# Attention stage of a two-layer graph network: one-hot products ahead of the sums on TensorE, weighing ahead of the logits on VectorE, the transposed one-hot made by ScalarE

## The chip, the cores and the metric

The kernel runs on one core of a Trainium2 chip. The metric is the device time of one execution, in microseconds (us); three executions of the kernel before lie between 6692.63 and 6696.04 us. The engines are TensorE (PE, with its weight loads as PEld), VectorE (DVE), ScalarE (ACT), GpSimd (POOL) and SyncE (SP), which only starts transfers. Each engine runs its own instructions strictly in the order in which they are written; they meet at semaphores alone.

## The reference, cut to what matters

Two graph layers run over 6250 nodes and 106250 edges that are sorted by their destination node. The change lies in the relational attention of the first layer:

```python
def rel_gat(W, a_s, a_d, b, mask):              # once for each of 4 edge types
    x = (node_inp @ W).reshape(N, H, D)         # H = 8 heads, D = 16
    es, ed = einsum(x, a_s), einsum(x, a_d)
    logit = leaky_relu(es[src] + ed[dst], 0.2)
    p = exp(logit - mx[dst]) * mask[:, None]    # mx: maximum over a node's edges
    den = segment_sum(p, dst)
    out = segment_sum(p / den[dst] * x[src], dst)
```

The kernel sums `p` and `p * x[src]` for each destination together and divides later.

## The kernel before

The program is a row of phases with a barrier behind each: `lists` (the schedule), `node_inputs`, `relation_maxima`, `node_maxima`, `relation_attention`, `node_update`, `edge_inputs`, `edge_messages`, `outputs`. The change is in `relation_attention` (L804 to L952), and there are two small moves in `lists` and `edge_inputs`.

`relation_attention` handles 1028 steps in 257 groups of four (`U` = 4). A step is one block of 128 edges against one window of 32 destination nodes; with 4 edge types a window has 128 keys (type and node), and an edge belongs to one key. `T.key` holds each edge's key. For a group j the engines do this:

- SP, `load` (L831): brings `keyrow` (the keys of the group's 512 edges, the same row in all 128 partitions) and four blocks of `xe` (source features and source logits).
- DVE, `spread` (L861): `keyT` = (`keyrow` equals the partition's number + 1), the transposed one-hot, 128 keys by 512 edges.
- PE, `expand` (L933): four products `keyT` by the window's row of `K.edm` (called `l_outside` in the trace, whose memory it reuses) into `dst_ps`: each edge gets its destination's logit and maximum. A product in float32 is two weight loads and two matmul passes in the trace, so a group has 8 of each.
- DVE, `select` (L867), in three steps: `logit` (L871), `leaky` (L874), `arg` (L879), reading `xe` and `dst_ps`.
- ACT, `exponentials` (L916): `p` = exp(`arg`) (L920). ACT also copies the group's keys (`keep`, L925), from which POOL makes the other one-hot, `keyhot` (L851).
- DVE, `weigh` (L881): `px` = `p` times `xe`.
- PE, `sums` (L943): four products `keyhot` by `px` into `sum_ps`.
- DVE, `add` (L890), once for each step: adds `sum_ps` to the window's row of `acc`.

Every engine's code is a loop over turns t. `pipeline(engine, groups, ring, [(skew, stage), ...])` makes a turn of the stages in the order of the list, each for group t minus its skew. So the order inside a turn is written by hand. Before, PE's turn is sums(t-3), expand(t-1). DVE's turn is written out in `tick` (L897): add(t-4, step 0), logit(t-2), add(t-4, 1), leaky(t-2), add(t-4, 2), arg(t-2), weigh(t-3), add(t-4, 3), spread(t-1). ACT's turn is keep(t), exponentials(t-2). Buffers between stages have four slots (`RG` = 4), the PSUM tiles `dst_ps` and `sum_ps` two.

Of the kernel before, what the change touches and what calls it, by code (L numbers as in the profile page):

```python
# [286 lines left out]
def lists(nc, K, T):  # L287

    with Phase(nc, "list") as ph:
# [54 lines left out]
        def _(sp):  # L344
# [18 lines left out]
            sp.wait_ge(s_st, 160)  # L363
            sp.wait_ge(s_made, KEY)
            sp.dma_start(T.key.rearrange("(p k) e -> p k e", k=KKC), key[:, :, :]).then_inc(s_st, 16)
            sp.wait_ge(s_st, 176)
# [437 lines left out]
def relation_attention(nc, K, T, acc):  # L804

    with Phase(nc, "att") as ph:
# [4 lines left out]
        keyrow = ph.sb("keyrow", [P, RG, U * P])  # L811
# [7 lines left out]
        px = ph.sb("px", [P, RG, U, XR])  # L819
# [3 lines left out]
        s_kr = [ph.sem(f"kr{b}") for b in range(RG)]  # L823
        s_key, s_kh, s_kT, s_dst, s_sc, s_arg, s_p, s_px, s_sum, s_acc = (
            ph.sem(n) for n in ("key", "kh", "kT", "dst", "sc", "arg", "p", "px", "sum", "acc"))
# [3 lines left out]
        @block.sync  # L829
        def _(sp):  # L830
            def load(j, b):  # L831
                e = registers(nc, sp, mybir.EngineType.SP, K.reg_ke, j * U, U, BLOCKS * P)
                if past(j, RG):
                    sp.wait_ge(s_kT, j - RG + 1)
                    sp.wait_ge(s_px, j - RG + 1)
                    settle(sp, K)
                sp.dma_start(keyrow[:, b, :], key[ds(j, 1), :].to_broadcast([P, U * P])).then_inc(s_kr[b], 16)
                for u in range(U):
                    sp.dma_start(xe[:, b, u, :], T.xe[ds(e[u], P), :]).then_inc(s_xe[b], 16)

            pipeline(sp, GROUPS, RG, [(0, load)])
# [15 lines left out]
        def _(dve):  # L857
# [23 lines left out]
            def weigh(j, b):  # L881
                dve.wait_ge(s_p, j + 1)
                if past(j, RG):
                    dve.wait_ge(s_sum, (j - RG + 1) * U)
                dve.scalar_tensor_tensor(px[:, b, :, :].rearrange("p u (h s) -> p (u h) s", h=H),
# [11 lines left out]
            def tick(t, h, has):  # L897
# [17 lines left out]
        def _(act):  # L915
# [11 lines left out]
            pipeline(act, GROUPS, RG, [(0, keep), (2, exponentials)])  # L927

        @block.tensor
        def _(pe):  # L930
# [303 lines left out]
def edge_inputs(nc, K, T, h1T):  # L1234

    with Phase(nc, "edgein") as ph:
# [10 lines left out]
        s_w, s_x, s_sd, s_norm, s_h, s_hT, s_hTs, s_ab, s_abs = (  # L1247
            ph.sem(n) for n in ("w", "x", "sd", "norm", "h", "hT", "hTs", "ab", "abs"))
# [473 lines left out]
def build(nc, T):  # L1722
# [4 lines left out]
    with Phase(nc, "k") as ph:  # L1727
# [6 lines left out]
        K.reg_w, K.reg_e = ph.sb("reg_w", [1, P * KC], I32), ph.sb("reg_e", [1, P * KC], I32)  # L1734
# [76 lines left out]
```

## Time and profile before

| what | value |
|---|---|
| median of 3 executions | 6694.62 us |
| the profiled execution's own time | 6689.12 us |
| its span, first to last instruction | 6686.9 us |
| attention loop, 1518.3 to 3013.8 us | 1495.5 us, 22% of the span |
| mean turn of the attention loop, 245 turns from 1560 to 2980 us | 1420 / 245 = 5.80 us |
| TensorE's granted clock in that loop | 0.50 of full speed |
| busy share there: PE, DVE, POOL, ACT | 64%, 45%, 40%, 7% |

All else in this document is taken from the profiled execution, which lies 5.5 us below the median of the timed ones; its own time is 2.2 us over its span. In the rows, a number in brackets at a row's end is the time for which the engine had been idle before it, with the instruction that released it. A wait for several semaphores is put down to whichever came last by the profile, so the name after `<-` can be a neighbour of the true one. Where two rows of one engine overlap, the second was issued before the first had drained.

### The profile page before, as it was taken

Reading aid. Unit: us, or ns where it says so; the run is one execution under the profiler, and the core shown is the slowest. Engines: PE = TensorE matmul, PEld = TensorE weight load, DVE = VectorE, ACT = ScalarE, POOL = GpSimd, SP = SyncE. Lnnn points to the kernel's source line nnn. Section 1 sums busy time; section 2 is a strip of 40 time slices with the busy share of each in tenths; the row PEclk is TensorE's granted clock in tenths of the full one; section 3 lists DMA queues with packets and bytes.
Section 4 is the critical chain, followed back from the end, with each engine's and each line's share of the span. In section 5 each row is a group of like instructions: output and inputs, shape, how many; then the busy total and the mean of one; then the engine's idle time right before and its main releaser. Section 6 shows DMA issues by size and latency. Waiting matters only on the chain. (4 is left out here: it accounts for less than half of the span.)

```text
span 6686.9 us, 101415 instructions
## 1 busy us (share of the span) xinstructions
PE 3841.0 (57%) x17939; PEld 2899.4 (43%) x17940; DVE 3444.8 (52%) x10929; ACT 898.4 (13%) x2786; POOL 4148.2 (62%) x3995
## 2 busy tenths in 40 slices
PE   0332222215666666662467777777677777777766
PEld 0221111115666666661434444444444444444446
DVE  4632222214444444448955665656566566556654
ACT  0210000000000000003331111111111111111111
POOL 3067777764444443434228888888888888888870
PEclk9855555555555555555688888888888888888888
DMA  1355555533333333332268788787778877787874
GB/s 49 117 137 145 142 145 145 145 83 97 95 96 96 97 97 96 95 89 101 50 181 169 165 170 169 165 170 167 168 165 169 170 167 169 169 167 166 171 151 127
DMA packets 917009, 908.21 MB, mean 136 GB/s; under 512 B 231003, under 2 KB 735099, under 8 KB 916759
## 3 DMA queue, kind: packets, MB, share of 16 engines
q0 software_dynamic: 238848, 434.00, 32.4%
q1 hardware_dynamic: 678119, 473.77, 26.3%
q14 instruction: 30, 0.25, 0.0%
q8 instruction: 12, 0.20, 0.0%
HBM read 656.68 MB, written 250.64 MB: 136 GB/s over the span
## 5 line engine op out<-in xcount | busy, mean ns | idle before, releaser
L1409 POOL DMA_INDIRECT sums<-msg_bsum,msg_sidx x928 | 1558.8, 1680 | 308.0 <-issue 268.9
L1551 PEld LDWEIGHTS msg_fwd_ps<-msg_onehot,msg_hid 128*128 128x128 f32 x3712 | 639.8, 224 | 1422.1 <-issue 1313.4
L1418 POOL DMA_INDIRECT msg_ga<-ab,msg_idx x928 | 951.4, 1025 | 390.7 <-issue 240.8
L851 POOL TENSOR_SCALAR att_keyhot<-k_ramp,att_keys 128x128 f32<-128x128 f32 x1028 | 602.3, 604 | 895.9 <-PE att_sum_ps L949 873.4
L1564 PE MATMUL msg_pre_ps<-msg_rw,msg_lt 128*128 128x512 f32 x1856 | 1110.2, 684 | 37.1 <-DVE msg_xs L1488 28.1
L1551 PE MATMUL msg_fwd_ps<-msg_onehot,msg_hid 128*128 128x64 f32 x3712 | 621.6, 298 | 819.0 <-DVE l_fwd L1470 814.3
L686 POOL DMA_INDIRECT max_xe<-rows,max_idx x832 | 800.1, 962 | 422.8 <-issue 253.3
L949 PE MATMUL att_sum_ps<-att_px,att_keyhot 128*128 128x136 f32 x2056 | 559.1, 454 | 537.4 <-DVE l_acc L895 521.5
L949 PEld LDWEIGHTS att_sum_ps<-att_px,att_keyhot 128*128 128x128 f32 x2056 | 478.3, 331 | 563.7 <-DVE l_acc L895 546.8
L1553 PE MATMUL msg_bwd_ps<-msg_hid,msg_same 128*128 128x256 f32 x1856 | 708.9, 469 | 0.0
L1522 ACT ACTIVATE msg_bsum<-msg_bwd_ps 128x256 f32<-128x256 f32 x928 | 356.2, 384 | 2564.5 <-PE msg_bwd_ps L1553 2550.1
L1495 DVE SCALAR_TENSOR_TENSOR msg_hid<-msg_xs 128x512 f32<-128x512 f32 x928 | 639.2, 689 | 0.1
L939 PEld LDWEIGHTS att_dst_ps<-l_outside,att_keyT 128*128 128x128 f32 x2056 | 473.8, 334 | 94.3 <-issue 94.3
L939 PE MATMUL att_dst_ps<-l_outside,att_keyT 128*128 x2056 | 444.4, 357 | 94.0 <-DVE att_keyT L865 94.0
L742 PE MATMUL max_mT_ps<-k_ident,max_m 128*32 128x128 f32 x832 | 194.0, 413 | 492.3 <-DVE max_m L699 492.3
L1487 DVE TENSOR_TENSOR msg_xs<-msg_pre_ps,msg_ga 128x256 f32<-128x256 f32 x928 | 390.6, 421 | 165.8 <-PE msg_pre_ps L1564 93.1
L895 DVE TENSOR_TENSOR l_acc<-l_acc,att_sum_ps 128x136 f32 x1028 | 303.1, 295 | 294.9 <-PE att_sum_ps L949 272.3
L1463 DVE TENSOR_SCALAR msg_sidx<-msg_rowf,k_trash 128x4 int32<-128x4 f32 x232 | 57.6, 248 | 760.5 <-DMA sums<-msg_bsum,msg_sidx 758.2
L1564 PEld LDWEIGHTS msg_pre_ps<-msg_rw,msg_lt 128*128 128x128 f32 x1856 | 388.1, 222 | 116.5 <-DVE msg_xs L1488 49.8
L1470 DVE TENSOR_TENSOR l_fwd<-l_fwd,msg_fwd_ps 128x128 f32 x928 | 261.5, 282 | 241.5 <-issue 224.9
L1488 DVE TENSOR_TENSOR msg_xs<-msg_pre_ps,msg_ga 128x256 f32<-128x256 f32 x928 | 385.2, 415 | 0.0
L712 DVE TENSOR_TENSOR_SCAN max_run<-max_begin,max_run,max_mT_ps 32x1024 f32<-32x1024 f32 x103 | 240.4, 2334 | 224.2 <-PE max_mT_ps L742 224.2
(260 smaller groups left out, 4807.6 us busy)
## 6 DMA issues: line engine op xcount, KB each, us to landing
msg_rw<-ab SPq DMA_DIRECT2D x928, 128.0 KB
att_xe<-xe SPq DMA_DIRECT2D x1028, 72.0 KB, 2.5
att_keyrow<-key SPq DMA_DIRECT2D x257, 256.0 KB, 3.5
xe<-max_xe SPq DMA_DIRECT2D x104, 576.0 KB, 3.5
msg_lt<-in_efT SPq DMA_DIRECT2D x928, 32.0 KB
msg_ga<-ab,msg_idx POOLq DMA_INDIRECT x928
sums<-msg_bsum,msg_sidx POOLq DMA_INDIRECT x928
rows<-node_rows SPq DMA_DIRECT2D x50, 288.0 KB, 2.4
```

The lines of the kernel that those rows point to most:

```text
L686: pool.indirect_dma_start(xe[:, b, u, :], None, T.rows, bass.IndirectOffsetOnAxis(ap=idx[:, b, u:u + 1], axis=0)).then_inc(s_xe[b], 16)
L851: pool.tensor_scalar(keyhot[:, b, u, :], K.ramp[:, 1:P + 1], keys[:, b, u:u + 1], None, ALU.is_equal).then_inc(s_kh, 1)
L939: last = pe.matmul(dst_ps[b % 2][:, u, :], keyT[:, b, u * P:(u + 1) * P], K.edm[:, ds(w[u], 1), :].rearrange("k a c -> k (a c)"), start=Tr ...
L949: pe.matmul(sum_ps[b % 2][u // 2][:, u % 2, :], keyhot[:, b, u, :], px[:, b, u, :], start=True, stop=True).then_inc(s_sum, 1)
L1409: pool.indirect_dma_start(T.sums[u % 2], bass.IndirectOffsetOnAxis(ap=sidx[:, b, u:u + 1], axis=0), bsum[:, b, u, :], None, compute_op=ALU ...
L1418: pool.indirect_dma_start(ga[:, b, u, :], None, T.ab, bass.IndirectOffsetOnAxis(ap=idx[:, b, u:u + 1], axis=0)).then_inc(s_ga[b], 16)
L1487: dve.tensor_tensor(xs[:, u % 2, 0:HID], pre_ps[u % 2][:, 0:HID], ga[:, b, u, HID:2 * HID], ALU.add)
L1488: dve.tensor_tensor(xs[:, u % 2, HID:2 * HID], pre_ps[u % 2][:, HID:2 * HID], ga[:, b, u, 0:HID], ALU.add).then_inc(s_x, 1)
L1495: dve.scalar_tensor_tensor(hid[:, b % 2, u, :], xs[:, u % 2, :], SLOPE1, xs[:, u % 2, :], ALU.mult, ALU.max).then_inc(s_hid, 1)
L1551: pe.matmul(fwd_ps[u % 2][:, q * WIN:(q + 1) * WIN], hid[:, b % 2, u, HID + q * P:HID + (q + 1) * P], onehot[:, b, u, :], start=True, stop ...
L1553: pe.matmul(bwd_ps[u % 2][:, :], same[:, b % 2, u, :], hid[:, b % 2, u, 0:HID], start=True, stop=True).then_inc(s_edge, 1)
L1564: pe.matmul(pre_ps[u % 2][:, :], lt[:, b, u, :], rw[:, b % 2, u, :], start=True, stop=True).then_inc(s_pre, 1)
```

## The change

1. PE's turn becomes expand(t-1), sums(t-3).
2. DVE's turn becomes add(t-4, 0), weigh(t-3), add(t-4, 1), logit(t-2), add(t-4, 2), leaky(t-2), add(t-4, 3), arg(t-2). `spread` is no longer on DVE.
3. ACT makes `keyT` in two passes: `away` = |part1 - keyrow|, then `keyT` = relu(1 - away), with the two biases read from a column of SBUF. The second waits for the first. ACT also issues the transfer of `keyrow`, which SP issued before. ACT's turn is load(t), keep(t), exponentials(t-2), spread(t-1).
4. `keyrow` and `px` have two slots in place of four, and `away` has one.
5. The tables `K.reg_w` and `K.reg_e` are loaded in `edge_inputs`, where they are next needed, and no longer in `lists`.

```diff
@@ lists, SP
-            sp.dma_start(K.reg_w[:, :], T.sched_w.rearrange("(a s) -> a s", a=1)).then_inc(s_st, 16)
-            sp.dma_start(K.reg_e[:, :], T.sched_e.rearrange("(a s) -> a s", a=1)).then_inc(s_st, 16)
@@ relation_attention, tiles
-        keyrow = ph.sb("keyrow", [P, RG, U * P])
+        keyrow = ph.sb("keyrow", [P, 2, U * P])
+        away = ph.sb("away", [P, U * P])
-        px = ph.sb("px", [P, RG, U, XR])
+        px = ph.sb("px", [P, 2, U, XR])
@@ SP, load
-                    sp.wait_ge(s_kT, j - RG + 1)
                     sp.wait_ge(s_px, j - RG + 1)
                     settle(sp, K)
-                sp.dma_start(keyrow[:, b, :], key[ds(j, 1), :].to_broadcast([P, U * P])).then_inc(s_kr[b], 16)
@@ DVE
-            def spread(j, b):
-                dve.wait_ge(s_kr[b], filled(j, b, RG, 16))
-                if past(j, RG):
-                    dve.wait_ge(s_dst, j - RG + 1)
-                dve.tensor_scalar(keyT[:, b, :], keyrow[:, b, :], K.part1[:, 0:1], None, ALU.is_equal).then_inc(s_kT, 1)
@@ DVE, weigh
-                if past(j, RG):
-                    dve.wait_ge(s_sum, (j - RG + 1) * U)
+                if past(j, 2):
+                    dve.wait_ge(s_sum, (j - 1) * U)
@@ DVE, tick
                 for u in range(U):
                     if has(4):
                         add(t - 4, slot(4), u, w[u])
-                    if has(2) and u < 3:
-                        select(t - 2, slot(2), u)
-                    if has(3) and u == 2:
+                    if has(3) and u == 0:
                         weigh(t - 3, slot(3))
-                if has(1):
-                    spread(t - 1, slot(1))
+                    if has(2) and u > 0:
+                        select(t - 2, slot(2), u - 1)
@@ ACT
-            pipeline(act, GROUPS, RG, [(0, keep), (2, exponentials)])
+            def load(j, b):
+                if past(j, 2):
+                    act.wait_ge(s_away, j - 1)
+                    settle(act, K)
+                act.dma_start(keyrow[:, b % 2, :], key[ds(j, 1), :].to_broadcast([P, U * P])).then_inc(s_kr[b % 2], 16)
+
+            def spread(j, b):
+                act.wait_ge(s_kr[b % 2], filled(j, b, 2, 16) if isinstance(j, int) else (j - b % 2) * 8 + 16)
+                if past(j, 1):
+                    act.wait_ge(s_kT, j)
+                act.activation(away[:, :], keyrow[:, b % 2, :], ACT.Abs, bias=K.part1[:, 0:1], scale=-1.0).then_inc(s_away, 1)
+                if past(j, RG):
+                    act.wait_ge(s_dst, j - RG + 1)
+                act.wait_ge(s_away, j + 1)
+                act.activation(keyT[:, b, :], away[:, :], ACT.Relu, bias=K.ones[:, 0:1], scale=-1.0).then_inc(s_kT, 1)
+
+            pipeline(act, GROUPS, RG, [(0, load), (0, keep), (2, exponentials), (1, spread)])
@@ PE
-            pipeline(pe, GROUPS, RG, [(3, sums), (1, expand)])
+            pipeline(pe, GROUPS, RG, [(1, expand), (3, sums)])
@@ edge_inputs, SP
+            sp.dma_start(K.reg_w[:, :], T.sched_w.rearrange("(a s) -> a s", a=1)).then_inc(s_reg, 16)
+            sp.dma_start(K.reg_e[:, :], T.sched_e.rearrange("(a s) -> a s", a=1)).then_inc(s_reg, 16)
```

How the built programs stand. ACT, one turn inside the attention loop, before: the copy of the keys, then the exponentials (L920) behind their wait for `att_arg`.

```order
L924 ISA
L925 ISA [waits att_kh]
L925 ACTIVATE att_keys<-l_key 128x4
L919 REGISTER_ALU [waits att_arg]
L920 ACTIVATE att_p<-att_arg 128x32 [waits att_px]
```

The same turn of ACT in the changed kernel:

```order
L920 ISA [waits att_away]
L920 DMA att_keyrow<-key 128x512
L913 REGISTER_ALU
L914 ISA [waits att_kh]
L914 ACTIVATE att_keys<-l_key 128x4
L909 ACTIVATE att_p<-att_arg 128x32 [waits att_px,att_arg]
L923 ISA
L926 ACTIVATE att_away<-att_keyrow,k_part 128x512 [waits att_kT,att_kr0]
L930 ACTIVATE att_keyT<-att_away,k_ones 128x512 [waits att_away,att_dst]
```

The two passes that make `keyT` stand behind the exponentials of the turn, and so behind their wait for `att_arg`.

PE, inside the loop, before: the wait for `att_px`, the four sums (L949), then the wait for `att_kT` and the first of four expansions (L939).

```order
L948 ISA [waits att_px,att_kh]
L949 MATMUL att_sum_ps<-att_px,att_keyhot 128x136 [waits att_acc] x2
L948 REGISTER_ALU
L949 MATMUL att_sum_ps<-att_px,att_keyhot 128x136 [waits att_acc] x2
L935 REGISTER_ALU
L939 ISA [waits att_arg,att_kT]
L939 MATMUL att_dst_ps<-l_outside,att_keyT 128x16
```

PE in the changed kernel, from the last expansion of a turn to the wait that opens the next turn:

```order
L944 ISA
L944 MATMUL att_dst_ps<-l_outside,att_keyT 128x16
L949 REGISTER_ALU
L953 ISA [waits att_px,att_kh]
L954 MATMUL att_sum_ps<-att_px,att_keyhot 128x136 [waits att_acc] x2
L953 REGISTER_ALU
L954 MATMUL att_sum_ps<-att_px,att_keyhot 128x136 [waits att_acc] x2
L940 REGISTER_ALU
L944 ISA [waits att_arg,att_kT]
```

The sums now stand behind the expansions of the same turn, and the wait for `att_kT` stands ahead of both.

DVE, one turn ahead of the loop, before:

```order
L895 TENSOR_TENSOR l_acc<-l_acc,att_sum_ps 128x136
L871 TENSOR_TENSOR att_logit<-att_xe,att_dst_ps 128x32 [waits att_xe1,att_dst]
L895 ISA [waits att_acc,att_sum]
L895 TENSOR_TENSOR l_acc<-l_acc,att_sum_ps 128x136
L874 SCALAR_TENSOR_TENSOR att_leaky<-att_logit 128x32 [waits att_sc]
L895 ISA [waits att_acc,att_sum]
L895 TENSOR_TENSOR l_acc<-l_acc,att_sum_ps 128x136
L879 TENSOR_TENSOR att_arg<-att_leaky,att_dst_ps 128x32 [waits att_p,att_sc]
L885 SCALAR_TENSOR_TENSOR att_px<-att_p,att_xe 128x544 [waits att_sum,att_p]
L895 ISA [waits att_acc,att_sum]
L895 TENSOR_TENSOR l_acc<-l_acc,att_sum_ps 128x136
L865 TENSOR_SCALAR att_keyT<-att_keyrow,k_part 128x512 [waits att_dst,att_kr2]
```

The same turn of DVE in the changed kernel:

```order
L886 ISA [waits att_acc,att_sum]
L886 TENSOR_TENSOR l_acc<-l_acc,att_sum_ps 128x136
L876 SCALAR_TENSOR_TENSOR att_px<-att_p,att_xe 128x544 [waits att_sum,att_p]
L886 ISA [waits att_acc,att_sum]
L886 TENSOR_TENSOR l_acc<-l_acc,att_sum_ps 128x136
L862 TENSOR_TENSOR att_logit<-att_xe,att_dst_ps 128x32 [waits att_xe1,att_dst]
L886 ISA [waits att_acc,att_sum]
L886 TENSOR_TENSOR l_acc<-l_acc,att_sum_ps 128x136
L865 SCALAR_TENSOR_TENSOR att_leaky<-att_logit 128x32 [waits att_sc]
L886 ISA [waits att_acc,att_sum]
L886 TENSOR_TENSOR l_acc<-l_acc,att_sum_ps 128x136
L870 TENSOR_TENSOR att_arg<-att_leaky,att_dst_ps 128x32 [waits att_p,att_sc]
```

`arg` is now DVE's last instruction of the turn, behind all four adds and the weighing.

## Rows read from the trace of the kernel before

**Rows 1.** Busy time in the stretch: length, PE, PEld, DVE, ACT, POOL, clock, DMA, GB/s.

```profile
1560.00:2980.00 1420.00, 904.89 (x3918) 879.87 (x3918) 632.71 (x2204) 95.53 (x490) 574.14 (x980) 0.50 0.36 96
```

**Rows 2.** Who waited for whom, 1560 to 2980 us: total us, times, longest.

```profile
ACT att_p L920 <- DVE att_arg L879: 1313.1, 245, 5.4
POOL att_keyhot L851 <- PE att_sum_ps L949: 846.9, 245, 3.6
PE att_sum_ps L949 <- DVE l_acc L895: 515.1, 245, 2.2
DVE att_logit L871 <- PE att_dst_ps L939: 507.2, 245, 2.1
```

**Rows 3.** One turn in order of time: start, length, engine, line, [idle before].

```profile
2207.40 0.48 DVE L865 TENSOR_SCALAR att_keyT<-att_keyrow,k_part 128x512 f32<-128x512 f32 x1
...
2207.52 1.86 PEld L949 LDWEIGHTS att_sum_ps<-att_px,att_keyhot 128*128 128x128 f32 x8 [2.29 <-DVE l_acc L895]
...
2208.94 0.30 DVE L895 TENSOR_TENSOR l_acc<-l_acc,att_sum_ps 128x136 f32 x1 [1.06 <-PE att_sum_ps L949]
2209.27 1.84 PEld L939 LDWEIGHTS att_dst_ps<-l_outside,att_keyT 128*128 128x128 f32 x8
...
2211.26 0.19 DVE L871 TENSOR_TENSOR att_logit<-att_xe,att_dst_ps 128x32 f32<-128x32 f32 x1 [2.02 <-PE att_dst_ps L939]
2211.47 0.29 DVE L895 TENSOR_TENSOR l_acc<-l_acc,att_sum_ps 128x136 f32 x1
2211.68 0.21 DVE L874 SCALAR_TENSOR_TENSOR att_leaky<-att_logit 128x32 f32<-128x32 f32 x1
...
2212.29 0.72 DVE L885 SCALAR_TENSOR_TENSOR att_px<-att_p,att_xe 128x544 f32<-128x544 f32 x1
2212.49 0.23 ACT L920 ACTIVATE att_p<-att_arg 128x32 f32<-128x32 f32 x1 [5.36 <-DVE att_arg L879]
2212.68 0.21 ACT L925 ACTIVATE att_keys<-l_key 128x4 f32 x1
2212.93 0.29 DVE L895 TENSOR_TENSOR l_acc<-l_acc,att_sum_ps 128x136 f32 x1
...
2213.22 0.33 SPq L837 DMA_DIRECT2D att_keyrow<-key  x1
2213.25 1.86 PEld L949 LDWEIGHTS att_sum_ps<-att_px,att_keyhot 128*128 128x128 f32 x8 [2.14 <-DVE l_acc L895]
```

**Rows 4.** ACT by group: shape, count, busy us, mean ns, idle before.

```profile
L1012 ACT ACTIVATE l_acc<-upd_tmp 128x512 f32 x44 | 27.7, 630 | 55.5 <-POOL upd_tmp L1003 55.5
L1308 ACT ACTIVATE edgein_h<-edgein_x,edgein_nmr,edgein_rstd 128x128 f32 x46 | 22.3, 484 | 0.0
L593 ACT ACTIVATE node_h<-node_x,node_rstd 128x128 f32 x46 | 18.0, 392 | 0.0
```

**Rows 5.** Timeline of the stage's start: keyT ahead of expansions, and logit ahead of leaky.

```profile
1522.35 0.88 DVE L865 TENSOR_SCALAR att_keyT<-att_keyrow,k_part 128x512 f32<-128x512 f32 x1 [4.46 <-DMA att_keyrow<-key]
...
1523.37 1.78 PEld L939 LDWEIGHTS att_dst_ps<-l_outside,att_keyT 128*128 128x128 f32 x8 [92.87 <-issue]
...
1528.49 0.19 DVE L871 TENSOR_TENSOR att_logit<-att_xe,att_dst_ps 128x32 f32<-128x32 f32 x1 [2.06 <-PE att_dst_ps L939]
1528.71 0.19 DVE L874 SCALAR_TENSOR_TENSOR att_leaky<-att_logit 128x32 f32<-128x32 f32 x1
```

**Rows 6.** Timeline of ACT in a later phase: an exponential and the instruction behind it.

```profile
3131.18 0.24 ACT L1203 ACTIVATE mix_ex<-mix_al 128x40 f32<-128x40 f32 x1 [2.36 <-DVE mix_al L1123]
3131.32 0.58 ACT L1187 ACTIVATE mix_gT<-mix_gT_ps 128x512 f32<-128x512 f32 x1
```

**Rows 7.** Timeline of the stage's end: an add that waits for the add before it.

```profile
3009.56 0.30 DVE L895 TENSOR_TENSOR l_acc<-l_acc,att_sum_ps 128x136 f32 x1 [0.21 <-DVE l_acc L895]
```

**Rows 8.** Timeline of the start of `edge_inputs`: ACT's first tile and its wait.

```profile
3352.94 0.88 ACT L1308 ACTIVATE edgein_h<-edgein_x,edgein_nmr,edgein_rstd 128x128 f32<-128x128 f32 x2 [12.92 <-DMA edgein_x<-x]
```

**Rows 9.** The page, transfers: tiles, queue, count, KB each, median us from issue to landing.

```profile
att_keyrow<-key SPq DMA_DIRECT2D x257, 256.0 KB, 3.5
```

More of the change, by code:

```diff
@@ L358, in _ @@
             settle(sp, K)
-            sp.dma_start(K.reg_w[:, :], T.sched_w.rearrange("(a s) -> a s", a=1)).then_inc(s_st, 16)
-            sp.dma_start(K.reg_e[:, :], T.sched_e.rearrange("(a s) -> a s", a=1)).then_inc(s_st, 16)
             sp.dma_start(K.reg_kw[:, :], T.ksched_w.rearrange("(a s) -> a s", a=1)).then_inc(s_st, 16)
             sp.dma_start(K.reg_ke[:, :], T.ksched_e.rearrange("(a s) -> a s", a=1)).then_inc(s_st, 16)
-            sp.wait_ge(s_st, 160)
+            sp.wait_ge(s_st, 128)
             sp.wait_ge(s_made, KEY)
             sp.dma_start(T.key.rearrange("(p k) e -> p k e", k=KKC), key[:, :, :]).then_inc(s_st, 16)
-            sp.wait_ge(s_st, 176)
+            sp.wait_ge(s_st, 144)
         @block.gpsimd
@@ L822, in relation_attention @@
         s_xe = [ph.sem(f"xe{b}") for b in range(RG)]
-        s_kr = [ph.sem(f"kr{b}") for b in range(RG)]
-        s_key, s_kh, s_kT, s_dst, s_sc, s_arg, s_p, s_px, s_sum, s_acc = (
-            ph.sem(n) for n in ("key", "kh", "kT", "dst", "sc", "arg", "p", "px", "sum", "acc"))
+        s_kr = [ph.sem(f"kr{b}") for b in range(2)]
+        s_key, s_kh, s_away, s_kT, s_dst, s_sc, s_arg, s_p, s_px, s_sum, s_acc = (
+            ph.sem(n) for n in ("key", "kh", "away", "kT", "dst", "sc", "arg", "p", "px", "sum", "acc"))
         block = ph.block()
@@ L882, in weigh @@
                 dve.wait_ge(s_p, j + 1)
-                if past(j, RG):
-                    dve.wait_ge(s_sum, (j - RG + 1) * U)
-                dve.scalar_tensor_tensor(px[:, b, :, :].rearrange("p u (h s) -> p (u h) s", h=H),
+                if past(j, 2):
+                    dve.wait_ge(s_sum, (j - 1) * U)
+                dve.scalar_tensor_tensor(px[:, b % 2, :, :].rearrange("p u (h s) -> p (u h) s", h=H),
                                          p[:, b, :, :].rearrange("p u h -> p (u h)").unsqueeze(2).to_broadcast([P, U * H, HW]),
@@ L948, in sums @@
                         pe.wait_ge(s_acc, (j - 2) * U + u // 2 * 2 + 2)
-                    pe.matmul(sum_ps[b % 2][u // 2][:, u % 2, :], keyhot[:, b, u, :], px[:, b, u, :],
+                    pe.matmul(sum_ps[b % 2][u // 2][:, u % 2, :], keyhot[:, b, u, :], px[:, b % 2, u, :],
                               start=True, stop=True).then_inc(s_sum, 1)
-            pipeline(pe, GROUPS, RG, [(3, sums), (1, expand)])
+            pipeline(pe, GROUPS, RG, [(1, expand), (3, sums)])
 def node_update(nc, K, T, acc):
@@ L1246, in edge_inputs @@
         ab_ps = [ph.ps(f"ab_ps{b}", [P, 2 * HID]) for b in range(2)]
-        s_w, s_x, s_sd, s_norm, s_h, s_hT, s_hTs, s_ab, s_abs = (
-            ph.sem(n) for n in ("w", "x", "sd", "norm", "h", "hT", "hTs", "ab", "abs"))
+        s_w, s_reg, s_x, s_sd, s_norm, s_h, s_hT, s_hTs, s_ab, s_abs = (
+            ph.sem(n) for n in ("w", "reg", "x", "sd", "norm", "h", "hT", "hTs", "ab", "abs"))
         s_st = [ph.sem(f"st{b}") for b in range(2)]
@@ L1268, in _ @@
                 sp.wait_ge(s_st[b], 16 * (TILES // 2))
+            sp.wait_ge(s_reg, 32)
         @block.vector
@@ L1733, in build @@
         K.headmask, K.trash = ph.sb("headmask", [P, H]), ph.sb("trash", [P, 1])
-        K.reg_w, K.reg_e = ph.sb("reg_w", [1, P * KC], I32), ph.sb("reg_e", [1, P * KC], I32)
         K.loc, K.src = ph.sb("loc", [P, P * KC]), ph.sb("src", [P, P * KC], I32)
@@ L1755, in build @@
             K.srcv, K.rowd = l1.sb("srcv", [P, STEPS]), l1.sb("rowd", [P, STEPS])
+            K.reg_w, K.reg_e = l1.sb("reg_w", [1, P * KC], I32), l1.sb("reg_e", [1, P * KC], I32)
             K.src_hl = l1.sb("src_hl", [P, STEPS, 2], BF16)
```

## The prediction

> **What bounds the kernel now.** I read the busy times of the attention loop first: between 1560 and 2980 us 245 turns take 1420 us, 5.80 us a turn, with PE busy 64%, DVE 45%, ACT 7%, and TensorE's granted clock at half speed, 1.2 GHz [rows 1]. No engine is full, so the stage goes by a ring of waits. The list of waits shows it: PE waits 2.1 us a turn for DVE (515.1 / 245), DVE waits 2.07 us for the expansions (507.2 / 245), ACT waits 5.4 us, POOL 3.5 us [rows 2]. The timeline gives the ring in four pieces [rows 3]: from the sums' first weight load to the expansions' 1.75 us (2207.52 to 2209.27), from there to the logit 1.99 (2211.26), from the logit to the weighing 1.03 (2212.29), from the weighing to the next sums' load 0.96 (2213.25). Together 5.73 us, the length of that turn. The wait of the sums is named after `l_acc`, but that add (2212.93) needs PSUM of the last turn only; the wait that the sums have to see is the one for `px`, written just before. So the ring is sums, expansions, logit, weighing, sums. What DVE does behind the weighing, the last add and the 0.48 us of `keyT` (2207.40), lies beside PE's 1.75 us and costs nothing.
>
> **The change, step by step.** I follow who waits for whom in the new order.
>
> Step 1: the old ring is cut. Sums(t-3) need px(t-3), which DVE now makes behind its first add, long before PE asks. Expand(t-1) stands ahead of them.
>
> Step 2: a new ring closes, through ACT. Expand(t-1) needs keyT(t-1). On ACT, spread(t-1) is queued behind exponentials(t-2), which wait for arg(t-2). That is now the last instruction of DVE's turn t. DVE's turn t begins with add(t-4, 0), which waits for the first two sums of group t-4, and these stand on PE behind expand(t-2). So expand(t-2), sums(t-4), DVE's whole turn, the exponentials, Abs, Relu, expand(t-1) follow one another with nothing beside them. Behind ACT's wait for `att_arg` the whole of `keyT` is queued, and PE's turn waits for that. Before, `keyT` needed nothing from ACT.
>
> Step 3: its length, from first weight load of the expansions to the next.
> - Expansions' load to the sums' load: eight loads took 1.75 us in the other order; with a semaphore wait between I take 1.80 (1.72 to 1.84, the loads' own 1.84 being the upper end) [rows 3].
> - Sums' load to the first add: 1.42 us (2207.52 to 2208.94), measured from an idle PE; behind running matmuls I add 0.08, a guess of mine within 0 to 0.18: 1.50 [rows 3].
> - DVE from the first add to the exponential's start: add to weigh 0.21 (as an add to `leaky`), weigh to add 0.64, add to logit 0.21, logit to exponential 1.23 (2211.26 to 2212.49): 2.29 [rows 3]. I allow 2.15 to 2.40.
> - Exponential to Abs: 0.14 in the later phase [rows 6]; there is a register instruction between, so 0.20 (0.14 to 0.43; the upper end is my allowance for the register work, twice the 0.21 of [rows 7]).
> - Abs and Relu: the trace has no 128x512 ACT instruction with a bias from SBUF. Without one it takes 0.630 us; a second such operand makes a 128x128 instruction 0.484 in place of 0.392, 0.092 more [rows 4]. So 0.72 each, between 0.63 and 0.81 (two operands).
> - Between the two, a wait for the engine's own result: no ACT row shows that. DVE's leaky starts 0.03 us after the logit's end (1528.49 + 0.19 to 1528.71) [rows 5], while an add that waits for the add before it starts 0.21 after it, with register work between [rows 7]. The loop's Relu is nearer to the first: 0.05.
> - Relu to the expansions' load: 1522.35 + 0.88 to 1523.37 is 0.14 [rows 5]; the sums came 0.24 behind the weighing's end (2212.29 + 0.72 to 2213.25) [rows 3]. I take 0.17.
>
> Sum: 1.80 + 1.50 + 2.29 + 0.20 + 0.72 + 0.05 + 0.72 + 0.17 = 7.45 us, against 5.80. That is 1.65 us more in each of 257 turns: +424 us. All low ends together give 1.72 + 1.42 + 2.15 + 0.14 + 0.63 + 0.03 + 0.63 + 0.14 = 6.86 us, +272; all high ends 1.84 + 1.60 + 2.40 + 0.43 + 0.81 + 0.21 + 0.81 + 0.24 = 8.34, +653. The sum says slower at either end.
>
> Step 4: the rest.
> - `keyT` off DVE: 0.48 us of DVE, which lay beside PE; worth nothing, and its cover isn't needed any more.
> - Adds 1 to 3 need no wait of their own: the second pair of sums ends some 0.9 us (half of 1.75) behind the first, and add 2 comes 0.21 + 0.64 + 0.21 + 0.21 = 1.27 us behind add 0.
> - `keyrow` from ACT: one DMA issue a turn, 0.33 us as SP has it [rows 3]. It stands ahead of the wait for `arg`, in which ACT idles 5.4 us a turn now [rows 2]. With the spread ACT's own work is some 0.33 + 0.21 + 0.23 + 1.44 = 2.2 us [rows 3], so over 4 us of idle time cover it. If that cover were gone, issue and key copy would cost 0.33 + 0.21 = 0.54 a turn. The transfer lands 3.5 us after its issue [rows 9] and is read a whole turn later.
> - Two slots of `keyrow` and `px`: weigh(t-3) asks for the sums of group t-5, done two turns before; load(t) for Abs of group t-2, done a turn before. No wait.
> - POOL: `keyhot` waits for the sums as before, 3.5 us idle a turn [rows 2], and is needed three turns later. SP loses an issue and a wait. Both free.
> - The two tables: in `lists` SP issues them ahead of its wait for `key`, which DVE makes much later; in `edge_inputs` they go out while ACT sits idle till 3352.94 for its input [rows 8]. Within 1 us either way.
>
> One rule weighed against the rows. DVE makes `keyT` in 0.48 us [rows 3], and ACT takes about 1.44 for its two passes by the sum above. The Trainium skill, page "ScalarE: Activation LUTs", section "Rules for kernel authors", says that relu and the like belong on VectorE and not on ScalarE. By that rule the move is a loss in itself; the rows agree in direction. Engine time alone costs nothing here, since ACT is 7% busy [rows 1]: what costs is the place in ACT's queue.
>
> So the profiled execution's own time, 6689.1 us, becomes 7113; the median of the timed ones lies 5.5 us above it, so I predict 7119 us.
>
> **The rivals.**
> - *TensorE becomes the bound* (the other side). If the spread of group t-1 ran ahead of ACT's wait for arg(t-2), PE would never wait: a turn would be 16 loads at 1.75 us for eight, 3.5 us, and 2.3 us a turn would go: 6695 - 257 x 2.3 = 6104 us. It decides at the point where Relu(t-1) ends before PE has finished the last turn's sums. For it: DVE's turn (2.3 us) and ACT's work (2.2 us) are both under 3.5. Against it: ACT runs in order, and the built order has both passes behind the wait. 3%.
> - *The granted clock rises to 2.4 GHz.* PE now runs 16 loads in one piece, as it did before (sums then expansions), but idles 3.9 us behind them in place of 2.3. The clock has stayed at 0.50 through the stretch at 64% busy [rows 1]; the new share is about 3.6 / 7.45, 48%. If it rose, PE's 3.30 us would halve: 5.80 us a turn, no change, 6695 us, and with the low ends for ACT (0.25 us less) 6631. The Trainium skill, page "TensorE: Matmul & The Clock Gate", section "What's actually happening", says that the idle state is the throttled one and activity releases it. By that rule less activity does not release what more did not. 6%, split between same and faster.
> - *ACT's transfer gets into the ring*, for instance where its issue stalls while the transfers of SP are in progress: 0.54 us a turn more, 7258 us. Against: 4 us of slack. 5%.
> - *The change does nothing measurable*, because a wait I take as satisfied holds the old ring in place: 2%, 6695 us.
>
> **How the numbers follow.** The forecast has 84%. The time is its own, 7119. From its ends: the low sum gives 6695 + 272 = 6967, the high one 7348, but it needs seven terms at their ends at once; I take 6960 to 7290, which leaves out a few per cent of the forecast, both clock cases and the bound by TensorE: somewhat under 2 in 10. Within 0.2% of the kernel before (about 13 us, what a measurement can tell) 5%, faster 5%, slower 90%.
>
> **What would show it.** In the profile after: a turn near 7.45 us and a stage near 1920; PE's idle time now ahead of the expansions, named after `keyT`, about 3.9 us a turn; none ahead of the sums; DVE's wait ahead of the first add (named after the sums) near 5 us a turn, none ahead of the logit; ACT's two 128x512 groups at 0.72 us each; the clock at 0.50. It would be wrong if PE waits for `att_px`, if ACT is not idle before the exponentials, or if the clock in that stretch is above 0.6.

## The result and the profile after

The changed kernel takes 7055.38 us (median of 4 executions, 7053.3 to 7064.98) against 6693.62 before (median of 4, one more than the three named at the start): a ratio of 1.0543, 95% interval 1.0525 to 1.0562. It is 362 us slower. The forecast was 7119 within 6960 to 7290, so the direction and the mechanism below held, and the size was 64 us too large.

Busy time in the attention loop after, where [rows 1] stood before; columns as there. Between 1560 and 3330 us 245 turns take 1770 us, 7.22 us a turn against 5.80. The turns are not all alike: from one group of expansions to the next they repeat in fours, 7.13, 7.17, 7.36 and 7.21 us. Further down, a turn is counted from the stage's first add to its last, divided by 257: 7.16 and 5.77 us. That takes in the ends of the stage, where not every engine has work for each group, and comes out a few hundredths shorter than the mean turn in the middle (5.80 and 7.22). From the first add to the last the stage grows from 1482 to 1840 us, 358 of the 362 us. PE falls from 64% to 54% busy, DVE from 45% to 28%, ACT rises from 7% to 25%; the clock stays at 0.50.

```profile
1560.00:3330.00 1770.00, 951.55 (x3920) 874.29 (x3920) 499.43 (x1962) 439.94 (x983) 575.08 (x983) 0.50 0.29 77
```

The waits there, for [rows 2]: total us, times, longest.

```profile
ACT att_p L909 <- DVE att_arg L870: 1280.2, 246, 5.6
DVE l_acc L886 <- PE att_sum_ps L954: 1230.4, 245, 5.2
PEld att_dst_ps L944 <- issue: 894.0, 245, 3.9
PE att_dst_ps L944 <- ACT att_keyT L930: 816.8, 245, 3.6
```

PE's wait is now ahead of the expansions (894.0 / 245 = 3.65 us a turn, named after `keyT`) and no longer ahead of the sums. DVE's wait has moved from the logit to the first add, and has grown from 2.07 to 5.02 us a turn. One turn in order of time, for [rows 3]:

```profile
2305.74 1.78 PEld L944 LDWEIGHTS att_dst_ps<-l_outside,att_keyT 128*128 128x128 f32 x8 [3.56 <-issue]
...
2307.40 1.91 PEld L954 LDWEIGHTS att_sum_ps<-att_px,att_keyhot 128*128 128x128 f32 x8
...
2308.86 0.30 DVE L886 TENSOR_TENSOR l_acc<-l_acc,att_sum_ps 128x136 f32 x1 [4.95 <-PE att_sum_ps L954]
2309.08 0.72 DVE L876 SCALAR_TENSOR_TENSOR att_px<-att_p,att_xe 128x544 f32<-128x544 f32 x1
...
2309.92 0.18 DVE L862 TENSOR_TENSOR att_logit<-att_xe,att_dst_ps 128x32 f32<-128x32 f32 x1
...
2310.87 0.18 DVE L870 TENSOR_TENSOR att_arg<-att_leaky,att_dst_ps 128x32 f32<-128x32 f32 x1
2311.08 0.23 ACT L909 ACTIVATE att_p<-att_arg 128x32 f32<-128x32 f32 x1 [5.29 <-DVE att_arg L870]
2311.24 0.72 ACT L926 ACTIVATE att_away<-att_keyrow,k_part 128x512 f32<-128x512 f32 x1
2312.05 0.72 ACT L930 ACTIVATE att_keyT<-att_away,k_ones 128x512 f32<-128x512 f32 x1
2312.66 0.34 ACTq L920 DMA_DIRECT2D att_keyrow<-key  x1
2312.90 1.78 PEld L944 LDWEIGHTS att_dst_ps<-l_outside,att_keyT 128*128 128x128 f32 x8 [3.60 <-issue]
```

Read it downwards: expansions, sums, first add, the rest of VectorE's turn to `arg`, exponential, Abs, Relu, the next expansions, 7.16 us from load to load. Each row starts where the one before lets it. This is the ring that the prediction drew. The logit (2309.92) stands 2.40 us behind the end of the expansions' weight loads (2305.74 + 1.78) and doesn't wait for them: it waits in VectorE's queue behind two adds and the weighing, and the first of these adds waits for the sums.

### The profile page after: what moved, and what is told of

Read it like the earlier page. It is cut to its first block and busy times, and to the rows that moved or that the text cites. A ratio compares the mean times of both kernels' runs of the same rounds, so it can differ in the third digit from the quotient of the medians.

```text
span 7063.1 us, 102365 instructions
## 1 busy us (share of the span) xinstructions
PE 3888.1 (55%) x17939; PEld 2893.2 (41%) x17940; DVE 3311.5 (47%) x10672; ACT 1258.6 (18%) x3300; POOL 4157.5 (59%) x3995
## 5 line engine op out<-in xcount | busy, mean ns | idle before, releaser
L944 PE MATMUL att_dst_ps<-l_outside,att_keyT 128*128 x2056 | 484.2, 376 | 944.4 <-ACT att_keyT L930 944.4
L944 PEld LDWEIGHTS att_dst_ps<-l_outside,att_keyT 128*128 128x128 f32 x2056 | 457.8, 328 | 1024.8 <-issue 1024.8
```

The costliest lines, as they stand in the source:

```text
L944: last = pe.matmul(dst_ps[b % 2][:, u, :], keyT[:, b, u * P:(u + 1) * P], K.edm[:, ds(w[u], 1), :].rearrange("k a c -> k (a c)"), start=Tr ...
```

## The experiments

All kernels keep the computation. "Turn" below is the time from the first to the last add of the stage divided by 257: 5.77 us before (1531.2 to 3013.4 us), 7.16 after (1536.4 to 3376.4).

| kernel | median us | kernel before beside it | ratio, 95% interval | turn us |
|---|---|---|---|---|
| changed kernel | 7055.4 | 6693.6 | 1.0543 (1.0525 to 1.0562) | 7.16 |
| act_spread_first | 6254.9 | 6694.2 | 0.9345 (0.9329 to 0.9361) | 4.06 |
| pe_sums_first | 6490.3 | 6694.2 | 0.9694 (0.9678 to 0.9710) | 4.95 |
| only_act_spread | 6702.3 | 6694.2 | 1.0011 (1.0001 to 1.0021) | 5.78 |
| only_dve_order | 6185.2 | 6694.2 | 0.9238 (0.9223 to 0.9254) | 3.77 |
| extra_in_front | 7385.5 | 6899.4 | 1.0703 (1.0680 to 1.0725) | 7.67 |
| extra_behind | 7245.3 | 6899.4 | 1.0504 (1.0485 to 1.0524) | 7.16 |
| dve_spread_last | 6936.2 | 6899.4 | 1.0049 (1.0033 to 1.0065) | 5.88 |
| act_two_turn_ring | 6344.3 | 6899.4 | 0.9197 (0.9178 to 0.9217) | 3.68 |
| only_pe_order | 6721.0 | 6699.0 | 1.0033 (1.0020 to 1.0047) | 5.86 |
| dve_spread_first | 6178.2 | 6699.0 | 0.9223 (0.9210 to 0.9235) | 3.74 |
| act_two_turn_ring_b | 6158.8 | 6699.0 | 0.9198 (0.9184 to 0.9212) | 3.68 |

The four from extra_in_front to act_two_turn_ring ran on another chip, on which the kernel before takes 6899 us. Their attention stages begin between about 1705 and 1730 us and not near 1519. The kernel of act_two_turn_ring was run again on a third chip as act_two_turn_ring_b, with the same turn, 3.68 us. So nearly all of the extra time lies ahead of the stage, and these kernels are compared with the kernel before on their own chip. The changed kernel itself was not run there.

### The place in ScalarE's queue: act_spread_first

```diff
-            pipeline(act, GROUPS, RG, [(0, load), (0, keep), (2, exponentials), (1, spread)])
+            pipeline(act, GROUPS, RG, [(0, load), (0, keep), (1, spread), (2, exponentials)])
```

> The changed kernel with one edit: in ScalarE's turn spread(t-1) stands ahead of exponentials(t-2). The theory (the time is lost because the two passes of keyT queue behind the wait for att_arg, which closes a ring of 7.15 us through PE, DVE and ACT once a turn): the ring now spans two turns, so TensorE's 16 weight loads (1.66 + 1.75 us) become the bound, 3.5 to 3.7 us a turn, about 6110 to 6170 us in all at half clock; if the clock rises with it, half the ring without PE's halves gives 2.8 us a turn, about 5925. The rival (ScalarE is slower at making keyT than VectorE, 1.44 us against 0.48, and that is what costs): hardly changed, 7000 to 7055.

Swapping two stages of one list takes the changed kernel from 7055 to 6255 us, 800 us, with all of ScalarE's work still there. The slow-engine rival is out. But 4.06 us a turn is more than the 3.5 to 3.7 expected. ScalarE in order of time in this run:

```profile
2305.00 0.23 ACT L909 ACTIVATE att_p<-att_arg 128x32 f32<-128x32 f32 x1 [2.05 <-DVE att_arg L870]
2305.21 0.34 ACTq L920 DMA_DIRECT2D att_keyrow<-key  x1
2305.75 0.20 ACT L914 ACTIVATE att_keys<-l_key 128x4 f32 x1 [0.52 <-POOL att_keyhot L848]
2305.86 0.71 ACT L926 ACTIVATE att_away<-att_keyrow,k_part 128x512 f32<-128x512 f32 x1
2306.66 0.72 ACT L930 ACTIVATE att_keyT<-att_away,k_ones 128x512 f32<-128x512 f32 x1
```

Load and keep now stand between the exponential and the next Abs: 0.86 us from one to the other (2305.00 to 2305.86) in place of 0.16. That puts the rival of the prediction, the transfer in the ring, into effect: it costs 0.70 there, where I had priced 0.54. The name POOL in the bracket is misleading: the 0.52 us of idle time are the issue of the DMA and its register work (the copy's own wait, in the program, is for GpSimd's work on the group four before it). The two-turn ring becomes 7.16 + 0.70 = 7.86 us, 3.93 a turn, of the 4.06 measured. The trace accounts for the rest: its turns repeat as 3.47, 4.43, 3.47 and 4.96 us, pairs of 7.90 and 8.43. The first pair is the sum above. In the second, ScalarE's loop, which holds four turns, goes back to its start between the exponential and Abs, and these two stand 1.33 us apart (2312.86 to 2314.19) in place of 0.86; the pair's extra 0.53 us is 0.13 a turn.

### The sums in the ring: pe_sums_first

```diff
-            pipeline(pe, GROUPS, RG, [(1, expand), (3, sums)])
+            pipeline(pe, GROUPS, RG, [(3, sums), (1, expand)])
```

> The changed kernel with TensorE's order of before (sums(t-3), expand(t-1)). The theory: the sums and the first adds leave the ring; what is left is expansions to logit 2.05, logit to exponential 1.15, exponential to the next expansions 0.14 + 0.71 + 0.09 + 0.72 + 0.14 = 1.80: 5.0 us a turn, 6490 us. The rival (the work of ScalarE alone costs the time, wherever PE's products stand): stays at 7055.

6490.3 us measured, 6490 expected. With TensorE's new order undone the sums and VectorE's first adds leave the ring, and the shorter one is left. One turn of it:

```profile
2303.03 1.78 PEld L944 LDWEIGHTS att_dst_ps<-l_outside,att_keyT 128*128 128x128 f32 x8 [1.40 <-issue]
...
2304.96 0.19 DVE L862 TENSOR_TENSOR att_logit<-att_xe,att_dst_ps 128x32 f32<-128x32 f32 x1 [2.49 <-PE att_dst_ps L944]
...
2306.10 0.23 ACT L909 ACTIVATE att_p<-att_arg 128x32 f32<-128x32 f32 x1 [3.02 <-DVE att_arg L870]
...
2307.07 0.72 ACT L930 ACTIVATE att_keyT<-att_away,k_ones 128x512 f32<-128x512 f32 x1
...
2307.92 1.78 PEld L944 LDWEIGHTS att_dst_ps<-l_outside,att_keyT 128*128 128x128 f32 x8 [1.32 <-issue]
```

Expansions to logit 1.93, logit to exponential 1.14, exponential to the next expansions 1.82: 4.89 us. The logit now waits for the expansions (2.49), as it did not in the changed kernel.

### The parts alone: only_act_spread, only_dve_order, only_pe_order

Only ScalarE's `keyT`, its transfer, the buffers and the moved tables (the changed kernel with both orders of before):

```diff
-                    if has(3) and u == 0:
-                        weigh(t - 3, slot(3))
-                    if has(2) and u > 0:
-                        select(t - 2, slot(2), u - 1)
+                    if has(2) and u < 3:
+                        select(t - 2, slot(2), u)
+                    if has(3) and u == 2:
+                        weigh(t - 3, slot(3))
...
-            pipeline(pe, GROUPS, RG, [(1, expand), (3, sums)])
+            pipeline(pe, GROUPS, RG, [(3, sums), (1, expand)])
```

> The changed kernel with the orders of before on TensorE and VectorE; of the change only ScalarE's keyT, its transfer and the smaller buffers are left. The theory: keyT is ready 1.66 us behind the exponential's start, 0.8 us before the expansions that follow the sums; the old ring of 5.80 us stands: 6694 us, within 15. The rival (ScalarE's slower arithmetic costs 1 us a turn): 6950.

8 us more at a ratio of 1.0011: within what was expected. Here the same two passes stand behind the same wait and cost nothing, since the expansions come behind the sums. ScalarE and the loads in this run:

```profile
2303.44 0.23 ACT L909 ACTIVATE att_p<-att_arg 128x32 f32<-128x32 f32 x1 [3.60 <-DVE att_arg L870]
2303.61 0.72 ACT L926 ACTIVATE att_away<-att_keyrow,k_part 128x512 f32<-128x512 f32 x1
...
2304.42 0.72 ACT L930 ACTIVATE att_keyT<-att_away,k_ones 128x512 f32<-128x512 f32 x1
...
2305.95 1.84 PEld L944 LDWEIGHTS att_dst_ps<-l_outside,att_keyT 128*128 128x128 f32 x8
```

`keyT` is done at 2305.14, 0.81 us before the expansions' first load.

Only VectorE's order, in the kernel before (`keyT` still last in VectorE's turn):

```diff
-                    if has(2) and u < 3:
-                        select(t - 2, slot(2), u)
-                    if has(3) and u == 2:
+                    if has(3) and u == 0:
                         weigh(t - 3, slot(3))
+                    if has(2) and u > 0:
+                        select(t - 2, slot(2), u - 1)
```

> The kernel before with VectorE's new order alone (weighing behind the first add, the logits one add later, keyT still last in VectorE's turn). The theory: weighing leaves the old ring; left are expansions to logit 2.05, logit to keyT's end 1.6, 0.14 to the next expansions: 3.8 us a turn, 6180 us; about 5920 if the clock rises. A rival (the new order of VectorE is itself part of the loss): 6700 or more.

6185.2 us against 6180 expected: the best part of the change is this one, and alone it would have been worth 509 us. Its busy times show TensorE nearly full:

```profile
1560.00:2450.00 890.00, 856.15 (x3756) 838.93 (x3757) 590.00 (x2115) 91.31 (x468) 574.57 (x940) 0.50 0.56 147
```

856 of 890 us is 96%, at half clock. That alone does not make TensorE the bound. Three turns of four take 3.57 to 3.71 us here, where the same products come down to 3.52 in the last kernels below; the ring through VectorE's `keyT` (3.8 us expected, 3.70 from one group of expansions to the next at 2306.70) is just longer than TensorE's own work.

Only TensorE's order, in the kernel before:

```diff
-            pipeline(pe, GROUPS, RG, [(3, sums), (1, expand)])
+            pipeline(pe, GROUPS, RG, [(1, expand), (3, sums)])
```

> The kernel before with TensorE's new order alone (expansions ahead of the sums). The theory: expansions to sums 1.66, to the first add 1.47, to the logit 0.21, to weighing 1.03, to the last add 0.64, to keyT 0.20, its 0.48 and 0.14 to the expansions: 5.83 us a turn, 0 to 40 us over the kernel before. The rival (TensorE's order alone brings the loss): 100 us or more over it.

22 us more, 5.86 us a turn against the 5.83 expected. So the parts give +8, -509 and +22 us, and together +362: the loss belongs to no part. It arises where the parts meet. Of the pairs, ScalarE's part with VectorE's order is pe_sums_first (204 us less than the kernel before), and both orders together are the next run; ScalarE's part with TensorE's order alone was not run.

### TensorE's and VectorE's orders without ScalarE: dve_spread_last

The kernel before with both new orders; VectorE makes `keyT` last in its turn.

```diff
+                    if has(3) and u == 0:
+                        weigh(t - 3, slot(3))
+                    if has(2) and u > 0:
+                        select(t - 2, slot(2), u - 1)
...
                 if has(1):
                     spread(t - 1, slot(1))
...
+            pipeline(pe, GROUPS, RG, [(1, expand), (3, sums)])
```

> The kernel before with both new orders, TensorE's and VectorE's, while VectorE still makes keyT, last in its turn. The theory (the ring is made by TensorE's order together with keyT behind the adds and logits, whichever engine makes it): 1.66 + 1.47 + 2.01 from first add to arg, 0.10 to keyT, 0.48 + 0.14 to the expansions: 5.86 us a turn, 6710 us (6690 to 6740). The rival (the orders are good and ScalarE spoils them): 3.5 to 4 us a turn, 6100 to 6230.

37 us over the kernel before, 5.88 us a turn (5.86 expected). The rival is out: with VectorE making `keyT` in 0.48 us the ring is still closed, and the 509 us of VectorE's order are lost just so.

```profile
2300.55 0.29 DVE L895 TENSOR_TENSOR l_acc<-l_acc,att_sum_ps 128x136 f32 x1 [3.27 <-PE att_sum_ps L949]
...
2302.64 0.48 DVE L865 TENSOR_SCALAR att_keyT<-att_keyrow,k_part 128x512 f32<-128x512 f32 x1
...
2303.26 1.78 PEld L939 LDWEIGHTS att_dst_ps<-l_outside,att_keyT 128*128 128x128 f32 x8 [2.28 <-issue]
...
2306.39 0.30 DVE L895 TENSOR_TENSOR l_acc<-l_acc,att_sum_ps 128x136 f32 x1 [3.26 <-PE att_sum_ps L949]
```

From `keyT`'s place in this kernel to ScalarE's in the changed one the ring grows from 5.88 to 7.16 us: the exponential and two passes of 0.72 in place of one of 0.48.

### The slope: extra_in_front and extra_behind

One more 128x512 pass of ScalarE a turn, into a tile that nothing reads:

```diff
+                act.activation(spare[:, :], K.key[:, 0:U * P], ACT.Copy)
                 act.activation(away[:, :], keyrow[:, b % 2, :], ACT.Abs, bias=K.part1[:, 0:1], scale=-1.0).then_inc(s_away, 1)
```

> The changed kernel with one more ScalarE pass a turn: a 128x512 copy of a constant tile into an unused one, between the exponential and Abs. The theory (everything that ScalarE does between the exponential and Relu lies in the ring): one pass of 0.63 us, overlapping its neighbour by 0.10, so 0.53 to 0.63 us more in each of 257 turns, 7190 to 7217 us. The rival (ScalarE is 25% busy and idles 5.2 us a turn, so a pass more costs nothing, and the change costs for another reason): 7055.

For the second kernel the same line stands behind Relu:

```diff
                 act.activation(keyT[:, b, :], away[:, :], ACT.Relu, bias=K.ones[:, 0:1], scale=-1.0).then_inc(s_kT, 1)
+                act.activation(spare[:, :], K.key[:, 0:U * P], ACT.Copy)
```

> The same extra pass of ScalarE, now behind Relu, at the end of its turn. The theory: it lies in ScalarE's idle time ahead of the next exponential, 5.2 us: 7055 us, within 15. The rival (ScalarE's engine time counts wherever it stands): as the other place, 7190 to 7217.

In front: 7385.5 us. Behind: 7245.3. The same work, 140 us apart (135 to 162 expected), or 7.67 against 7.16 us a turn; behind Relu the turn is that of the changed kernel to the hundredth. The totals can't be set against the expected 7055 us, which was for the first chip: over the kernel before on its own chip extra_behind is 346 us slower, where the changed kernel on the first is 362. That the pass behind Relu costs nothing rests on the turn. ScalarE of the first and of the second:

```profile
2302.55 0.23 ACT L910 ACTIVATE att_p<-att_arg 128x32 f32<-128x32 f32 x1 [5.37 <-DVE att_arg L871]
2302.70 0.63 ACT L927 ACTIVATE att_spare<-l_key 128x512 f32<-128x512 f32 x1
2303.24 0.71 ACT L928 ACTIVATE att_away<-att_keyrow,k_part 128x512 f32<-128x512 f32 x1
```

```profile
2301.61 0.23 ACT L910 ACTIVATE att_p<-att_arg 128x32 f32<-128x32 f32 x1 [4.88 <-DVE att_arg L871]
2301.78 0.72 ACT L927 ACTIVATE att_away<-att_keyrow,k_part 128x512 f32<-128x512 f32 x1
2302.59 0.72 ACT L931 ACTIVATE att_keyT<-att_away,k_ones 128x512 f32<-128x512 f32 x1
```

The pass in front delays Abs from 0.17 to 0.69 us behind the exponential, and the kernel by 0.51 us a turn. Behind Relu it comes out of the idle time ahead of the exponential, which is 5.29 us in the changed kernel and 4.88 here.

### Versions that keep the gain: act_two_turn_ring, dve_spread_first

The changed kernel with TensorE's order of before, and ScalarE's turn with `spread` ahead of the exponentials and `keep` at the end:

```diff
-            pipeline(act, GROUPS, RG, [(0, load), (0, keep), (2, exponentials), (1, spread)])
+            pipeline(act, GROUPS, RG, [(0, load), (1, spread), (2, exponentials), (0, keep)])
...
-            pipeline(pe, GROUPS, RG, [(1, expand), (3, sums)])
+            pipeline(pe, GROUPS, RG, [(3, sums), (1, expand)])
```

> The changed kernel with TensorE's order of before, and ScalarE's turn as load, spread, exponentials, keep. The theory: keyT waits for the exponential of the turn before, so the ring of 5.0 us and 0.5 us for the transfer's issue spans two turns, 2.75 us each; TensorE's 16 loads, 1.66 + 1.75 us, are the bound: 3.4 to 3.55 us a turn, 6080 to 6115 us at half clock. If another wait is left: as the run that had spread first, 4.0 us, 6230.

The ratio is 0.9197; at 3.68 us a turn it is 0.13 to 0.28 above what I expected of the loads alone. Where that comes from stands at the end of this section. The other version, on the kernel before with VectorE's new order:

```diff
                 if has(4):
                     w = windows.of(t - 4, slot(4))
+                if has(1):
+                    spread(t - 1, slot(1))
...
-                if has(1):
-                    spread(t - 1, slot(1))
```

> The kernel before with VectorE's new order and keyT made first in VectorE's turn, ahead of the adds; TensorE's order of before, nothing on ScalarE. The theory: keyT then needs the arg of the turn before only, all rings span two turns, and TensorE's 16 weight loads (1.66 + 1.75 us) are the bound: 3.45 to 3.65 us a turn, 550 to 600 us less than the kernel before, a ratio of 0.91 to 0.92. If VectorE is the bound (four adds, weighing, three small ones, keyT: 2.6 us): not seen as long as TensorE stays at half clock; at full clock 2.7 us a turn, 800 us less.

> The same kernel as the run with load, spread, exponentials, keep on ScalarE, beside the version that makes keyT on VectorE, on one chip. The theory: both are held by TensorE, so both lie within 30 us of one another; if ScalarE's wait for the keyrow transfer counts, this one is 20 to 60 us slower.

6178.2 and 6158.8 us: within 30 us of one another, and the one on ScalarE is 19 us ahead with no overlap of their ranges (6153 to 6166, 6173 to 6184). Both beat the kernel before and the changed one; the faster is 8.0% under the kernel before and 12.7% under the changed one. Busy times of the ScalarE version, then of the VectorE version with one of its waits:

```profile
1560.00:2400.00 840.00, 809.90 (x3637) 804.05 (x3637) 481.86 (x1820) 415.78 (x910) 602.19 (x910) 0.50 0.60 151
```

```profile
1560.00:2400.00 840.00, 795.24 (x3571) 789.48 (x3571) 556.40 (x2009) 87.05 (x446) 554.75 (x894) 0.50 0.58 148
...
DVE att_keyT L865 <- issue: 89.7, 56, 1.6
```

TensorE is 96% and 95% busy. The VectorE version missed its 3.65 us a turn by 0.09, and its ratio (0.9223) can't be told from that of only_dve_order (0.9238). Their traces show what sets the turns. The ScalarE version in order of time:

```profile
2309.19 1.84 PEld L944 LDWEIGHTS att_dst_ps<-l_outside,att_keyT 128*128 128x128 f32 x8
2310.91 1.91 PEld L954 LDWEIGHTS att_sum_ps<-att_px,att_keyhot 128*128 128x128 f32 x8
2312.71 1.84 PEld L944 LDWEIGHTS att_dst_ps<-l_outside,att_keyT 128*128 128x128 f32 x8
...
2313.99 0.29 DVE L886 TENSOR_TENSOR l_acc<-l_acc,att_sum_ps 128x136 f32 x1 [1.71 <-PE att_sum_ps L954]
...
2315.18 1.86 PEld L954 LDWEIGHTS att_sum_ps<-att_px,att_keyhot 128*128 128x128 f32 x8 [0.63 <-DVE l_acc L886]
...
2316.93 1.84 PEld L944 LDWEIGHTS att_dst_ps<-l_outside,att_keyT 128*128 128x128 f32 x8
```

The first turn takes 3.52 us, 1.72 from the expansions' loads to the sums' and 1.80 from there on, and TensorE waits for nothing. Three turns of four are like it, in both versions: here TensorE is the bound. The expectations had 1.66 + 1.75 us for it, two figures that were taken with TensorE idle just before. The second turn takes 4.22 us, and each fourth is like it: VectorE comes late to its first add, the weighing behind it is late too, and the sums wait 0.63 us. (In the VectorE version that turn takes 4.50.) The waits of TensorE ahead of the sums in 840 us, of the ScalarE version and of the VectorE version (total us, times, longest), and an instruction of the VectorE version (count, ns: least, median, most; first and last start):

```profile
PEld att_sum_ps L954 <- DVE l_acc L886: 36.0, 57, 0.6
...
PEld att_sum_ps L949 <- DVE l_acc L895: 50.5, 56, 1.0
...
L141 DVEq TENSOR_LOAD <-l_reg_kw x56: 1096/1102/1116, 1561.1 to 2389.1; - x56
```

In one turn of four VectorE reads the next sixteen window numbers from SBUF into registers, which takes 1.10 us and stands ahead of everything else in its turn. After it the sums wait 0.63 us in the ScalarE version and 0.90 in the VectorE version, where `keyT` stands between the reading and the first add. The difference, 0.27 us in one turn of four, is 17 us over 257 turns: about the 19 by which the ScalarE version is ahead. It is also why `keyT` at the start of VectorE's turn gained so little over only_dve_order: three turns of four became shorter (3.52 us for 3.57 to 3.71), and the fourth longer (4.50 for 4.21). No run leaves the reading out or moves it, so this is read from the traces and not tested. ScalarE waits for its transfer of `keyrow` in 124 of some 227 turns (85.4 us) in its version; TensorE has work meanwhile, and it costs nothing that shows.

## Why the prediction was right

**The old ring is cut (step 1)**: right. TensorE no longer waits ahead of the sums, and only_dve_order shows the size of it, 5.77 to 3.77 us a turn. **A new ring through ScalarE (step 2)**: right, and shown from four sides. Taking `keyT` out from behind the exponential gives back 800 us; taking the sums out gives back 565; ScalarE's part alone costs 8 us; a pass more costs 0.51 us a turn inside the ring and nothing outside it.

**Its length (step 3)**: too long. The mean turn is 7.22 us, and the sum said 7.45. Term by term, the turn shown above (7.16 us, one of the shorter ones) against the sum: expansions to sums 1.66 for 1.80; sums to first add 1.46 for 1.50; first add to exponential 2.22 for 2.29; exponential to Abs 0.16 for 0.20; Abs 0.72 for 0.72; to Relu 0.09 for 0.05; Relu 0.72 for 0.72; Relu to expansions 0.13 for 0.17. The differences add up to 0.29 us in this turn; for the mean turn it is 0.23, or 59 us over 257 turns, about the 64 by which the time came out shorter. The largest is the first term, 0.14 us: I gave the expansions the sums' pace of 1.75 us for eight loads and an allowance for a wait. Behind an idle TensorE the expansions take 1.66, and the wait behind them is already satisfied and adds nothing to that. The mistake was to add allowances to terms that the rows gave as they are: of the additions of 0.05, 0.08, 0.06 and 0.03 us the turn shows 0.00, 0.04, 0.02 and 0.00. Seven of the eight terms were too long or right and one too short (the gap between Abs and Relu), so little of the agreement is owed to errors that cancel. (The prediction speaks of seven terms at their ends; its sum has eight.)

**The rest (step 4)**: right. The transfer's issue by ScalarE (0.34 us) falls into idle time that is 5.2 us long, as the prediction had it; act_spread_first shows what it costs when that cover is gone, 0.70 us together with the key copy against 0.54 priced. Its median time to land is 3.3 us (3.5 before), and nobody waits for it. The smaller buffers cost nothing that only_act_spread can show.

```profile
att_keyrow<-key ACTq DMA_DIRECT2D x257, 256.0 KB, 3.3
```

**The rivals.** TensorE as the bound did not come about in the changed kernel, but its point of decision was nearly the right one. With `keyT` ahead of ScalarE's wait, act_two_turn_ring_b comes to 6159 us where the rival said 6104. It has TensorE's order of before as well. With the move of `keyT` alone (act_spread_first) the time is 6255 us: the sums are still in the ring, and its 7.90 us over two turns are more than TensorE's 2 x 3.52. The clock did not rise. Of the marks that I set, VectorE's wait near 5 us (5.02), the two groups at 0.72 us (0.718 and 0.721), no wait ahead of the logit and the clock at 0.50 are met; TensorE's idle time is 3.65 us a turn for 3.9, and the stage 1858 us long for 1920.

## What to carry to other kernels

Where engines run in order, price a reordering by the longest ring, one turn of work that must end before the next can start: write down for each stage what it waits for and what is queued in front of it, and follow it back to itself. Three edits that are harmless or good one by one (+8, -509, +22 us) can close such a ring together (+362). Work put on an idle engine is free only if it is not queued behind a wait for the very work that it feeds; the cure is its place in the engine's turn, so that the ring spans two turns. And once an engine is the bound, look at the turns one by one: here three of four are at TensorE's 3.52 us, and the fourth makes the mean 0.18 to 0.25 us longer.

## What the runs showed of the hardware

TensorE's clock stayed at half speed, the lower of its two levels (1.2 and 2.4 GHz), through the attention stage even where it was 96% busy for 890 us (only_dve_order) and 840 us (act_two_turn_ring_b), with clock 0.50 in both rows above. In the kernel before, between 4000 and 6500 us, it is 72% busy at a mean granted clock of 0.85:

```profile
4000.00:6500.00 2500.00, 1798.19 (x8298) 1214.54 (x8296) 1501.37 (x5279) 397.36 (x1131) 2038.61 (x1507) 0.85 0.80 168
```

So the stretch with the lower busy share had the higher clock. The Trainium skill, page "TensorE: Matmul & The Clock Gate", section "What's actually happening", says that the clock follows how busy the engine has recently been; these rows do not bear that out. Why they differ is open.

At that lower clock, eight weight loads of 128x128 in float32 with their products take 1.66 us (16 columns) and 1.75 us (136 columns) when TensorE was idle before them, and 1.72 and 1.80 us when it was not (act_two_turn_ring_b).

ScalarE's two passes (1.44 us) did not lose against VectorE's one (0.48 us) once both stood in the right place: 6158.8 against 6178.2 us. The Trainium skill, page "ScalarE: Activation LUTs", section "Rules for kernel authors", gives relu to VectorE. The case's rows agree on the engine's time, 0.48 against 1.44 us for the whole tile, though VectorE makes it by a comparison and not by relu; the kernel is still faster without it there.

GpSimd's 128x128 comparison takes 601 ns in the changed kernel and 679 ns on average in act_two_turn_ring_b. It is still no bound (602 of 840 us), and its cause was not looked for.

```profile
L848 POOL TENSOR_SCALAR att_keyhot<-k_ramp,att_keys 128x128 f32<-128x128 f32 x910 | 603.0, 679 | 237.8 <-ACT att_keys L914 237.8
```
